# GpSimd waits for the landing of the last gather issued, ahead of every second block of gathers, in a deformable residual block with attention

## What is computed

```python
def deform_conv(x, off, w):                      # off comes from two 3x3 convolutions of x
    py = arange(H) + DY + off[:, :, 0];  px = arange(W) + DX + off[:, :, 1]     # 9 taps per pixel
    y0, x0 = floor(py), floor(px);       wy, wx = py - y0, px - x0
    def corner(yi, xi, wgt):
        valid = (yi >= 0) & (yi < H) & (xi >= 0) & (xi < W)
        idx = clip(yi, 0, H - 1) * W + clip(xi, 0, W - 1)
        return x_flat[:, :, idx] * (wgt * valid)
    cols = corner(y0, x0, (1 - wy) * (1 - wx)) + corner(y0, x0 + 1, (1 - wy) * wx) \
         + corner(y0 + 1, x0, wy * (1 - wx)) + corner(y0 + 1, x0 + 1, wy * wx)
    return einsum('nckhw,ock->nohw', cols, w)
out = relu(batchnorm(deform_conv(x, off1, w1)))
out = relu(batchnorm(deform_conv(out, off2, w2)) + x)
q, k, v = projections(out);  out = gamma * (v @ softmax(q @ k, axis=1)) + out
```

## Time and profile before

| what | us |
|---|---|
| median of three runs | 781.89 |
| lowest and highest run | 781.34, 785.77 |
| profiled execution, span from first to last instruction | 930.4 |
| busy: PE, DVE, ACT, POOL | 773.5, 597.9, 501.1, 483.8 |
| POOL, gathers (L538), 440 of them | 475.9 |

### The profile page before, as it was taken

One profiled execution on the slowest core, in us unless ns is written; L12 is line 12 of the kernel. 1 busy time (PEld: TensorE's weight loads), 2 busy tenths in 40 slices (PEclk: granted clock), 3 DMA queues, 4 the chain that ended last, 5 costly groups with the idle time before them and its releaser, 6 DMA issues.

```text
span 930.4 us, 12479 instructions
## 1 busy us (share of the span) xinstructions
PE 773.5 (83%) x3497; PEld 469.0 (50%) x3497; DVE 597.9 (64%) x1605; ACT 501.1 (54%) x1269; POOL 483.8 (52%) x458
## 2 busy tenths in 40 slices
PE   7288798996879876973978979797887989989997
PEld 7245464553445443462536535353443544467887
DVE  4175579685657663952956868485665668876752
ACT  2174566665646563635655647474555555666432
POOL 3647557676667666325766657576667652000000
PEclk7579899997999988975989979898999889899999
DMA  6727646655565546336476555565555551000001
GB/s 213 253 80 226 193 137 179 182 149 148 150 190 158 148 139 189 92 111 206 142 225 180 156 152 150 151 171 157 159 170 172 160 156 57 1 1 1 24 24 46
DMA packets 55104, 130.14 MB, mean 140 GB/s; under 512 B 8271, under 2 KB 24944, under 8 KB 55036
## 3 DMA queue, kind: packets, MB, share of 16 engines
q0 software_dynamic: 35200, 115.37, 42.4%
q1 hardware_dynamic: 19820, 13.94, 4.8%
q10 hardware_dynamic: 16, 0.03, 0.0%
HBM read 118.76 MB, written 10.55 MB: 139 GB/s over the span
## 4 chain that ended last, share of the span: by engine, by line
PE 51%; another core or an unknown queue 17%; ACT 11%; DVE 10%; issue 9%; DMA 1%; DVEq 0%; ACTq 0%; SPq 0%
PE pair L1334 16%; PE pair L1347 6%; PE bank L1489 4%; ACT V L620 4%; ACT U L622 3%; PE bank L1285 3%; PE bank L1287 3%; PE pair L1320 3%; DVE V L926 2%; DVE U L926 2%; PE pair L1339 2%; PE pair L1449 2%; PE pair L1424 2%; DVE ST L976 2%
## 5 line engine op out<-in xcount | busy, mean ns | idle before, releaser
L538 POOL DMA_INDIRECT G<-table,rowi x440 | 475.9, 1082 | 292.3 <-DVE U L926 143.8
L1334 PE MATMUL pair<-ST,XT 128*128 128x512 f32 x544 | 270.6, 631 | 13.2 <-issue 9.6
L976 DVE TENSOR_TENSOR ST<-pair,stacks 128x512 f32<-128x512 f32 x180 | 119.7, 685 | 103.1 <-remote 83.6
L620 ACT ACTIVATE V<-G,wgt 128x128 f32<-128x128 f32 x440 | 175.0, 398 | 0.7 <-DMA G<-table,rowi 0.3
L622 ACT ACTIVATE U<-G,wgt 128x128 f32<-128x128 f32 x440 | 172.7, 393 | 0.0
L1334 PEld LDWEIGHTS pair<-ST,XT 128*128 128x128 f32 x544 | 109.8, 204 | 119.5 <-issue 96.8
L689 ACT COPY CT<-bank 128x512 f32<-128x512 f32 x110 | 64.3, 584 | 184.8 <-remote 116.2
L926 DVE SCALAR_TENSOR_TENSOR V<-G,wgt,V 128x128 f32<-128x128 f32 x440 | 152.4, 346 | 3.8 <-issue 3.8
L926 DVE SCALAR_TENSOR_TENSOR U<-G,wgt,U 128x128 f32<-128x128 f32 x440 | 152.7, 347 | 0.0
L1285 PE MATMUL bank<-band,V 128*128 128x128 f32 x440 | 105.6, 287 | 54.6 <-issue 31.7
L976 DVE TENSOR_TENSOR ST<-bank,stacks 128x512 f32<-128x512 f32 x92 | 63.0, 685 | 126.8 <-remote 97.1
(11 more groups left out here) (173 smaller groups left out, 769.3 us busy)
## 6 DMA issues: line engine op xcount, KB each, us to landing
table<-XT SPq DMA_DIRECT2D x16, 512.0 KB, 4.5
G<-table,rowi POOLq DMA_INDIRECT x440
out_dram<-G SPq DMA_DIRECT2D x8, 256.0 KB, 2.0
X<-in_x_dram SPq DMA_DIRECT2D x3, 512.0 KB, 6.5
A<-in_L_conv_dcn_w_dram SPq DMA_DIRECT2D x2, 576.0 KB
X<-in_x_dram SPq DMA_DIRECT2D x2, 256.0 KB, 2.9
table<-zeros SPq DMA_DIRECT2D x4, 16.0 KB, 2.1
qkv_nat<-in_L_conv_wv_dram SPq DMA_DIRECT2D x1, 64.0 KB
```

The costliest lines, as they stand in the source:

```text
L538: pool.indirect_dma_start(G[:, i % UNITS, r, :], None, table(n).rearrange("r (e k) -> r e k", e=2), bass.IndirectOffsetOnAxis(rowi[:, at:a ...
L620: act.activation(V[:, i % V_RING, r, :], G[:, i % UNITS, r, 0:C], ACT.Copy, scale=wgt[:, tile:tile + 1, 0])
L976: dve.tensor_tensor(ST[:, all_y % ST_RING, :], sel_acc[all_y % SEL_RING], HX[:, d % 2, :], ALU.mult).then_inc(st_ready[l], 1)
L1334: pe.matmul(dense_acc, XT[:, g // IGROUPS * TS + t, :], ST[:, all_y % ST_RING, :], start=(t == 0), stop=(t == QT - 1)).then_inc(dense_mm[l ...
```

## The change

Ahead of every second block from block 2 on (i = 2, 4, ... 54 in each layer) POOL waits until the last gather of the block before has landed, which is the last gather that it has issued. A nop follows the wait. Nothing else is changed.

```diff
                         for m in range(n, N if n else 1):
                             pool.wait_ge(table_out[l][m], 16 * 2)
                         pool.nop(nofuse=True)
+                    if i and i % 2 == 0:
+                        pool.wait_ge(gathered[(i - 1) % UNITS][GTILES - 1], gathers(l, i - 1))
+                        pool.nop(nofuse=True)
                     for r in range(GTILES):
                         if i >= UNITS:
                             pool.wait_ge(corner[l], GTILES * (i - UNITS) + r + 1)
```

## The result

The changed kernel takes 941.9 us (median of 4 runs, 939.1 to 944.4), the kernel before 781.7: a ratio of 1.205 (95% interval 1.201 to 1.209), 160 us slower. The forecast was 908, its range 830 to 945.

A forecast was written before the change was run, and what follows sets the result against it. The prediction took POOL's chain of gather issues to be as long as the timed run, with little spare time. 781.9 + 156.6 for 54 waits - 30 of spare time = 908.5, forecast 908 us, range 830 to 945.

The forecast's parts named there:

- POOL's own sum: Gathers and their gaps, start, wait for row numbers and attention add to 786.6 us without a wait for a buffer.
- the stops of the unknown releaser: Pauses in the first profile's chain, 153.5 us in 31 pieces over both layers; taken as mostly absent in timed runs.
- 30 to 50 us come through: Added waits carried through the first profile: most of 157 us vanish into POOL's 143.8 us of waits for DVE.
- The price of a wait: At each of 54 places on POOL's queue: 2.9 us, from 0 to 3.2; 156.6 us in all.
- the landing: Time from POOL finishing a gather until it lands, read from the DMA share: 2.2 us.
- The release: Time from the end of the awaited DVE instruction to POOL's next gather: 0.75 us.
- I take 30 us: Spare time on POOL in timed runs that hides part of the added waits: 30 us, between nothing and 143.8.
- (c): Rival: waits drain the DMA queue and shorten long gathers, saving up to 59.7 us; 762 us; chance 0.02.
- The cross-check: From POOL alone, its 786.6 us plus 156.6 us of added waits: 943 us at the row's pace.
- What is late next: ACT's scaling at L620 would wait for gathers, tens of microseconds in place of 0.3 us.
- (a): Rival: POOL has room because profiling stretches its 1.25 us per gather; about 810 us (790 to 830); chance 0.10.
- (b): Rival: DVE's release of the buffer comes after the landing anyway, so waits cost nothing; 782 us; chance 0.03.

The follow-up runs named there:

- second profile: The unchanged kernel before, profiled once more in a single run: 784.5 us, span 782.7 us.
- Experiment 9: The changed kernel with the fourth gather of each odd block left out (54 gathers), the third one's data used instead: 877.5 us.
- experiment 6: The kernel before with the fourth gather of each odd block left out, the third one's data used instead: 770.4 us, ratio 0.988.
- experiment 5: The kernel before run once more, unchanged, for its profile, the second profile: 784.5 us, span 782.7 us.
- experiment 2: The change with its wait ahead of every fourth block in place of every second, 26 waits: 862.3 us, ratio 1.102 against the kernel before.
- disturbed execution: The first profiled execution of the unchanged kernel before, used by the prediction: span 930.4 us, with stops of an unnamed releaser.
- experiment 1: The change with its 54 waits made for the last gather of the block before the previous one: 782.8 us, ratio 1.001 against the kernel before.
- 10: The change, waiting for the first gather of the block before in place of the last: 786.2 us, ratio 1.008 against the kernel before.
- experiment 11: The kernel before with four big DVE steps of the hats reading one tensor in place of two, results wrong: 772.5 us, ratio 0.989.

## Why the prediction was right, and where its sizes were off

- *What bounds.* Right, against the page's busy shares. POOL's own sum, 786.6 us without a wait for a buffer, was put beside the median of 781.9 and gave the answer that POOL has no room. The second profile shows it: no wait over 0.3 us for a buffer. Experiment 9 does so for the changed kernel, which gives back 0.95 us for each microsecond of POOL's issue that is left out. The kernel before does not (experiment 6): there PE is only 10 us behind, which the prediction did not say.
- *"So I take it that the stops of the unknown releaser are mostly absent in the timed runs."* Right (experiment 5), though I took them for something that a profile brings, and so expected them in the next profile: 955 to 985 us for the changed kernel's span. It is 938.1. The walk through the trace that gave "30 to 50 us come through" was a walk through the stops, and told nothing of the timed runs.
- *The price of a wait*, 2.9 us and at most 3.2, is the term that was mis-sized: it is 3.37 on average (3.24 in the example above), which makes 182.2 us of the 156.6. The step in it that failed is the landing. I read it off where the DMA share falls to nothing, 2.2 us after POOL's part, and that end of the packets was read rightly (2.3 in the example). But POOL waits for the semaphore, which rises 2.85 us after POOL's part on average at the 54 places, 0.65 more. The release was right: 0.75 us from the earlier trace rows and 0.1 for the second wait and nop, 0.80 measured together. The first gather after a wait for a landing is not longer (0.94 us in the middle, where I had added 0.16), and that took back part of the error. 2.85 + 0.80 - 0.30 = 3.35, against the 3.34 of the gaps at these places.
- *"I take 30 us"* of spare time on POOL. The number fits and the reason does not. POOL had none: its longest wait for a buffer is 0.3 us, and experiment 2 would have shown a reserve first and did not. What comes off has the form of rival (c)'s saving: long gathers get rarer, 459.4 to 432.1 us, 27.3. Whether a drained queue is the reason, as (c) has it, is not shown. That this came near the 30 I had put in is luck.
- *The sum.* 54 x 3.37 - 27.3 = 154.7 us against my 156.6 - 30 = 126.6; the 28 us between them are nearly all the price of the wait (25.6). The medians differ by 160, the two profiles by 155. The cross-check, 943 us at the row's pace and without a reserve, came closest because its errors cancel: its price of the waits is 25.6 us too low, and the 27.3 us of shorter gathers are missing.
- *What is late next.* ACT's scaling, as said: it waits 238.8 us. The 0.3 us beside it belongs to the disturbed execution, though; in the second profile of before ACT waits 66.1 us, 109 times.
- *Rivals.* (a), room on POOL from a slower pace under a profile: no, the median gather takes 946 to 949 ns in the profiles, disturbed or not. (b), the wait is met anyway: only where it is made for an earlier gather (experiment 1, and at most places 10). (c) had a saving of real size in it, 27 us, but without room on POOL it can't outweigh 182. Its condition was stated rightly.
- *The estimate from a page.* The Trainium skill's page "DMA: Bandwidth & Descriptors", section "Anatomy of one DMA — SWDGE (gpsimd) path", gives an estimate of 2.6 us for 256 KB; the trace has 2.3 us from the end of POOL's part to the last transfer in the example, 2.85 us on average from there to the landing at the 54 places, and 3.7 us from issue to landing. By that estimate in place of 2.2 the price of one wait would have been 3.3, near the measured 3.34: I kept the lower figure of the DMA share, and it was the estimate that was closer.

## What to carry to other kernels

An engine that issues DMAs is full when the start-to-start time of its issues fills the stage, whatever its busy share says; here 1.25 us, 0.95 busy and 0.30 of gap, 440 times. On such an engine a wait for the transfer just issued costs, each time, what is left until its landing and the time to go on (3.3 us here), and waiting for one issued three places earlier costs next to nothing. A landing is the rise of the semaphore, and the DMA share falls to nothing before it (by 0.5 us here). And before a profile is used to judge slack, its span should be held against the timed runs: when it is far longer, what looks like slack may exist only in that execution.

## What the runs showed of the hardware

- *Landing and going on.* In the example the DMA share falls to nothing 2.3 us after POOL's part and the semaphore has its value after 2.74 us. With the change ACT starts 0.02 us after the landing that it waited for (236 times alike), POOL's next gather 0.80 us after it (0.74 to 0.81 at the 54 places), with one more wait and nop in between.
- *A met wait is free.* In experiment 1 54 waits and nops cost nothing that can be measured (ratio 1.001, 0.998 to 1.004).
- *Long gathers.* Most gathers take 946 ns on POOL, some two to three times as long. With POOL idle more often their excess over 440 x 0.946 = 416.2 us falls, from 43 us (second profile of before) to 16 (the change) and 19 (every block); with shorter DVE steps that read one tensor it falls to 26. In the second profile of before 31 gathers take over 1.3 us, and 24 of them lie beside one of the four steps that experiment 11 replaces. The Trainium skill's page "SBUF — State Buffer", section "SBUF: two separate sides", tells of a port that VectorE and GpSimd share and of a VectorE operation in a mode with two ports that keeps GpSimd from writing descriptors. Experiment 11 agrees so far that DVE's work beside a gather matters, 43 us of excess against 26; no run shows the mode of a step, and which kind of step does it is not settled.
- *PE's clock follows POOL.* The mean granted clock is 0.959 in the second profile of before, 0.902 with the change and 0.862 with a wait ahead of every block. PE is idle for over 2 us in one piece 6, 24 and 53 times in these profiles, and the clock stands at the lower of its two levels, 1.2 GHz, in 7 stretches (66 us in all), 27 (185 us) and 47 (309 us). One of them in the changed kernel: PE is idle from 269.7 to 275.2, the granted clock falls to 0.50 at 273.9 and is at 1.00 again from 280.7. In the changed kernel this costs no time of its own, since nothing of it comes back to POOL: the buffer of each gather is free at least 8.9 us before it.
